# ACT fetches eight tiles instead of six in each plain run of a graph network, in bursts of six and sixteen rows

## The reference

```
edge_index = jnp.stack([src, dst])
x = _layernorm(x + _L0_gnn_ref(edge_index, x, edge_type_8, ...), axis=-1)   # message: row of x @ weight[type]
x = _layernorm(x + _L1_gnn_ref(x, edge_index, ...), axis=-1)                # message: row of x; unit length, batch norm
x = _layernorm(x + _L2_gnn_ref(x, src, dst, ...), axis=-1)                  # three attention layers, 4 heads
x = _layernorm(x + _L3_gnn_ref(x, L3_gnn_W, edge_index), axis=-1)           # message: row of (x @ W) * norm
# each message passing: agg = jax.ops.segment_sum(table[src], dst, num_segments=6250)
```

## Time and profile before

| | |
|---|---|
| median of 3 runs | 6618.36 us (6616.93 to 6622.67) |
| profiled execution | 6617.75 us, span 6615.8 us |
| busy: PE, DVE, ACT, POOL | 72%, 68%, 43%, 70% |
| run a0, first gather to last | 384.2 to 1335.4 us |
| run a1 | 1352.1 to 2301.0 us |
| run a5 | 5650.2 to 6600.5 us |

### The profile page before, as it was taken

One profiled execution on the slowest core, in us unless ns is written; L12 is line 12 of the kernel. 1 busy time (PEld: TensorE's weight loads), 2 busy tenths in 40 slices (PEclk: granted clock), 3 DMA queues, 4 the chain that ended last, 5 costly groups with the idle time before them and its releaser, 6 DMA issues. The chain is left out here.

```text
span 6615.8 us, 117241 instructions
## 1 busy us (share of the span) xinstructions
PE 4732.4 (72%) x16858; PEld 2811.9 (43%) x16858; DVE 4465.7 (68%) x11724; ACT 2869.6 (43%) x11409; POOL 4598.1 (70%) x4869
## 2 busy tenths in 40 slices
PE   9977777767677757777675777775776777667666
PEld 4445555533344334444443444443444444333333
DVE  5146555555555578888887888886888888655555
ACT  3310000000000058888875888885788887000000
POOL 0057777767777637777777777777777777677776
PEclk9988888778888777878886878877787778777777
DMA  6444444433333345555545555554455554344443
GB/s 207 158 138 123 123 123 122 122 108 109 110 109 109 106 149 141 143 143 142 144 111 139 143 144 142 143 145 147 136 142 144 143 141 114 103 116 116 115 115 107
DMA packets 448959, 865.75 MB, mean 131 GB/s; under 512 B 125022, under 2 KB 275447, under 8 KB 448219
## 3 DMA queue, kind: packets, MB, share of 16 engines
q0 software_dynamic: 227728, 627.54, 34.9%
q1 hardware_dynamic: 175408, 190.99, 9.0%
q10 hardware_dynamic: 45082, 39.73, 1.9%
HBM read 755.74 MB, written 102.10 MB: 130 GB/s over the span
## 5 line engine op out<-in xcount | busy, mean ns | idle before, releaser
L671 POOL DMA_INDIRECT rows_a<-table,rows_src x2454 | 2348.1, 957 | 874.7 <-issue 528.6
L891 PE MATMUL ps<-rows_a,hot_a 128*128 x4980 | 1865.2, 498 | 767.7 <-DMA rows_a<-table,rows_tile_a 411.2
L2080 ACT ACTIVATE rows_a<-rows_a,ex_a 128x64 f32<-128x64 f32 x9588 | 2320.8, 336 | 0.0
L2157 PE MATMUL ps<-rows_a,hot_a 128*128 128x260 f32 x4908 | 1815.9, 490 | 157.6 <-DVE agg L1989 144.3
L806 DVE TENSOR_TENSOR agg<-agg,ps 128x256 f32 (+1 forms) x2490 | 1046.0, 420 | 1203.5 <-PE ps L891 1136.5
L736 POOL DMA_INDIRECT rows_a<-table,rows_tile_a x1460 | 1383.7, 948 | 445.4 <-issue 253.2
L891 PEld LDWEIGHTS ps<-rows_a,hot_a 128*128 128x128 f32 x4980 | 1026.3, 237 | 1530.0 <-DVE agg L806 847.0
L1989 DVE TENSOR_TENSOR agg<-agg,ps 128x260 f32 x2490 | 1039.0, 417 | 320.3 <-PE ps L2157 134.1
L2157 PEld LDWEIGHTS ps<-rows_a,hot_a 128*128 128x128 f32 x4908 | 975.4, 230 | 446.9 <-issue 339.9
L736 POOL DMA_INDIRECT rows_a<-table,row x759 | 721.0, 950 | 231.7 <-issue 154.5
L2092 PE MATMUL ps<-ident,el_a 128*64 128x128 f32 x156 | 57.1, 366 | 518.1 <-DVE fac_a L1976 505.7
(11 more groups left out here) (354 smaller groups left out, 4126.9 us busy)
## 6 DMA issues: line engine op xcount, KB each, us to landing
rows_a<-table SPq DMA_DIRECT2D x6528, 1.0 KB
dstt_a<-dloc_dram SPq DMA_DIRECT2D x156, 512.0 KB
own_a<-table SPq DMA_DIRECT2D x4608, 1.0 KB
table<-ob SPq DMA_DIRECT2D x48, 1024.0 KB, 4.5
rows_a<-table,rows_src POOLq DMA_INDIRECT x2454
rows_a<-table ACTq DMA_DIRECT2D x2304, 1.0 KB
rows_a<-table,rows_tile_a POOLq DMA_INDIRECT x1460
table<-ob_n SPq DMA_DIRECT2D x98, 130.0 KB, 2.9
```

Of the source, the lines that this page charges most:

```text
L671: nc.gpsimd.indirect_dma_start(out=rows[:, n % ring, 0:width], out_offset=None, in_=table, in_offset=bass.IndirectOffsetOnAxis(ap=index[:, ...
L891: nc.tensor.matmul(ps[n % banks][:, 0:width], hot[:, m % nbuf, j, :], mine[n % 4], start=True, stop=True).then_inc(step_done, 1)
L2080: ins = nc.scalar.mul(a, a, ex[:, k % GV, s, h:h + 1])
L2157: nc.tensor.matmul(ps[j % banks][:, 0:W4], hot[:, j, :], step_rows(k, j), start=True, stop=True).then_inc(step_done, 1)
```

## The change

ACT gets eight tiles a run instead of six: every 98th from tile 84, not every 128th from tile 100. The tiles go over 12 bursts each, of 6 and 16 rows in turn (22 rows a block; the last burst of a tile has 12). Ten bursts (five blocks' worth, 110 rows) are issued ahead of the first block, not four (64 rows). In each block a burst of six stands in the middle of ACT's part, handed in as a function to the `act` methods: in a0 between the copies L974 and L978, in a1 between root and second square, in a5 between the first store and the wait for it. The burst of 16 stays behind the block. SP loads ACT's lists of row numbers at other places between its tiles, two more lists a run.

```diff
-ACT_TILE = 128
-ACT_FIRST = 100
+ACT_TILE = 98
+ACT_FIRST = 84
 ACT_TILES = tuple(range(ACT_FIRST, T - 1, ACT_TILE))
 ACT_PLACES = 2
-BURST = 16
-BURSTS_AHEAD = 4
+BURSTS = tuple((22 * b + lo, min(22 * b + hi, P)) for b in range(-(-P // 22)) for lo, hi in ((0, 6), (6, 22)))
+BLOCKS_AHEAD = 5
...
                     if i >= 2:
-                        sp.wait_ge(asked, P // BURST * (i - 1))
+                        sp.wait_ge(asked, len(BURSTS) * (i - 1))
...
-                    if ready < len(ACT_TILES) and i == (ACT_TILE * (ready - 1) + ACT_FIRST) // OWN_TILE - 1:
+                    if ready < len(ACT_TILES) and i == (ACT_TILES[ready - 2] + P // 2) // OWN_TILE:
                         ask_index_of_act(ready)
...
-                    i, lane = q * BURST // P, q * BURST % P
+                    i, (lane, end) = q // len(BURSTS), BURSTS[q % len(BURSTS)]
...
-                    ask_rows(act, mybir.EngineType.Activation, act_index[:, i % 2], lane, lane + BURST, BURST, octets, 4 * D,
+                    ask_rows(act, mybir.EngineType.Activation, act_index[:, i % 2], lane, end, end - lane, octets, 4 * D,
                              table.shape[0] - 1, rows[:, TRING + OWN_PLACES + place, 0:D], act_full[place])
                     act.sem_inc(asked, 1)
-                for _ in range(BURSTS_AHEAD):
+                for _ in range(2 * BLOCKS_AHEAD):
                     burst(0)
                 for i in range(NB):
-                    after.act(act, i)
+                    after.act(act, i, burst)
                     burst(done_by(i))
...
             nc.scalar.copy(self.xt[:, 1].rearrange("p h e -> p (h e)"), ps[4][:, 0:2 * P]).then_inc(self.xt_c, 1)
+            burst(done_by(i))
             act.wait_ge(self.l_done, i + 1)
...
             nc.scalar.sqrt(self.length[:, 0:1], self.ss[:, i:i + 1]).then_inc(self.rooted, 1)
+            burst(step)
             act.wait_ge(self.centred, i + 1)
...
                           self.ob[LAST:P, u]).then_inc(self.tail_out, 16)
+            burst(done_by(i))
             act.wait_ge(self.tail_out, 16 * (i + 1))
```

More of the change, by code:

```diff
@@ L824, in _ @@
                 after.act_first(act)
-                bursts = iter(range(len(ACT_TILES) * P // BURST))
+                bursts = iter(range(len(ACT_TILES) * len(BURSTS)))
                 def burst(done):
@@ L964, in act_x, with act @@
             nc.scalar.copy(self.xt[:, 0].rearrange("p h e -> p (h e)"), ps[4][:, 0:2 * P]).then_inc(self.xt_x, 1)
-        def act(self, act, i):
+        def act(self, act, i, burst):
             u = i % 2
```

## The result

The changed kernel takes 6645.89 us (median of 7 runs, 6640.75 to 6650.23), the kernel before 6622.42 in the runs beside them (6616.93 to 6623.02): a ratio of 1.0039, with a 95% interval of 1.0029 to 1.0049. That is 19 to 32 us slower, where +2 was forecast and 6632 was the upper end of the range. The profiled execution took 6645.88 us, 28.1 more than that of before.

What follows compares the result with a forecast made beforehand. POOL's gathers, 1.253 us a tile, were taken as the bound. Six gathers fewer (-7.5) plus stalls of 8.1, 1.4 and 0 gave +2.0 us: 6619.8 for the profiled execution, 6620.4 for the median, range 6610 to 6632.

Steps and rivals of the forecast that it cites:

- the price of the bursts ahead of block 0: ACT before its first block: ten bursts take 49.5 us, making its work 22 us later (17 to 25) in each run.
- the stalls that were worked out: POOL at tile 59 or 60 waits for PE's steps: 8.1 us in a0, 1.4 in a1, 0 in a5.
- Two gathers a run leave POOL: POOL fetches two tiles fewer in each of three runs: 6 x 1.253 = 7.5 us saved, all on the path.
- Root 0 of a0 near 448: ACT's first root in a0 moves from 426.29 to 448.3 behind the longer first bursts.
- From root 0 to the copy 9.5 us: In a0, ACT's copy of the next x follows root 0 by 9.5 us, at 457.8.
- From the copy to root 1 5.7: In a0, the burst behind the copy has 12 rows: 7.0 - 4 x 0.33 = 5.7 us, root 1 at 463.5.
- Bursts inside the blocks cost nothing: Six more rows a block, 3.0 us on ACT, are covered by its idle time in each run.
- The low clock: The longer hold starts PE at granted clock 0.50 (1.2 GHz); at full clock a0's 9.5 would be 8, stall 6.6.
- The hold is long in all three runs: Rival, 0.12: at the lower clock released PE catches up nothing; stalls 27.5 less 7.5 give +20 us, 6638.
- ACT becomes the bound: Rival, 0.07: the burst of six lifts ACT's part of a block over 19.4 us; about +33 us, 6651.
- The hold is swallowed: Rival, 0.17: DVE and PE catch up before tile 59 or 60, no stall; -7.5 us, 6611.
- More is gained than two tiles a run: Rival, 0.04: gathers get cheaper as POOL shares less; over 13.2 us needs 2.5 ns on each of 2271 gathers.

Runs made afterwards that it cites:

- Experiment 1: The changed kernel with bursts cut at multiples of four row numbers, 112 rows ahead instead of 110; ratio 1.0005 to the kernel before, +3.3 us.
- experiment 2: The changed kernel with three blocks' worth of bursts ahead (66 rows) instead of five, cuts unchanged; ratio 0.9986 to the kernel before, -9.3 us.
- experiment 3: The changed kernel with both three blocks' worth ahead (68 rows) and cuts at multiples of four; ratio 0.9985 to the kernel before, -10 us.
- experiment 6: 68 rows ahead and cuts at multiples of four, but both bursts of a block behind its part, none in its middle; ratio 0.9985 to the kernel before.
- experiment 7: Nine ACT tiles a run, ten bursts a tile cut at multiples of four, 52 rows ahead; ratio 0.9979 to the kernel before, 6619.25 against 6632.85 us.
- experiment 4: The kernel before with seven bursts of 16 ahead (112 rows) instead of four, six tiles, none in mid-block; ratio 1.0010, +6.6 us.
- experiment 5: The changed kernel with bursts cut at 5 and 22 instead of 6 and 22, 110 rows ahead; ratio 1.0069 to the kernel before, +46 us.

## Why the prediction was wrong

**The step that failed** is the price of the bursts ahead of block 0: "Five of each are 5 x 6.9 + 5 x 3.0 = 49.5, so the first block's work of ACT comes 22 us later (17 to 25 by the two bounds)". It measured 59.6, 32 us more than before. The 6.9 was that of bursts that start at multiples of 16, and I carried it over to bursts of the same length that start at 6, 50 and 94, where a burst takes 9.2 to 9.5 us (5684.17 to 5693.64 and 5707.44 to 5716.67 in the chain above). The bounds varied only the burst of six and held the other fixed, so the upper bound was no bound. The small bursts were under-priced too: taken at 3.0, with 2.0 and 3.6 as the bounds and 2.6 as another estimate, they took 3.2 to 3.8 in a5 (5680.89 to 5684.17, 5693.64 to 5697.47 above), as loads of six alone take 0.95 to 1.59. In a0 the five long bursts took 41.3 us in place of 34.5 and the five small ones 18.3 in place of 15.

**The rest of the sum stands.** Ten us more of hold on the stalls that were worked out (8.1, 1.4 and, behind 2 us of slack, 0) give 18, 11.5 and 8, in all 37.5; measured were 17.4, 13.2 and 5.1, in all 35.7. The 5.1 is less than 8 mostly because block 0 of a5 took 14.4 us from root to root (5739.81 to 5754.19 above), where 16.5 was taken. Experiment 1, where the ten bursts last the 50 us that I had taken, gives 7.7, 3.0 and 0 and +3.3 us (-2.7 to +9.3) against the forecast +2. In detail:
- Two gathers a run leave POOL: right, 757 are left and the gaps are still 1.25.
- Root 0 of a0 near 448: it came at 460.22. In experiment 1 it came at 448.20.
- From root 0 to the copy 9.5 us: 7.9. From the copy to root 1 5.7: 7.0, the same as before. In both traces the root is released by DVE (6.62 <-DVE mv_a, here and in the earlier trace rows) and not by the burst, so four rows fewer saved nothing. The prediction had read that 7.0 as the burst's own length, and its 1.65 for the reading of the numbers held a wait for DVE too. The two errors nearly cancel, 14.9 for 15.2: that is luck.
- The stall sits at tiles 59 and 60 and nowhere else: right. Most of it sat at tile 59, not 60.
- Bursts inside the blocks cost nothing: right, as far as these intervals tell (experiments 2, 3 and 6).
- The low clock: from 432 to 461 PE was busy for 0.32 us and was granted 0.50 (1.2 GHz), in the first row of the view below; in the 19 us behind it was granted 0.85 as a mean, in the second. The Trainium skill (TensorE: Matmul & The Clock Gate, Part 1) has it as a rule that activity releases the throttle; the trace agrees. But the way was 7.9 us and not 11.7 or more.

The busy time by stretch in a0 of the changed kernel (us, busy time of the engines, then granted clock, DMA share and GB/s):

```profile
432.00:461.00 29.00, 0.32 (x1) 0.00 (x0) 0.45 (x3) 1.58 (x2) 20.58 (x22) 0.50 0.41 110
461.00:480.00 19.00, 16.71 (x61) 12.27 (x62) 13.90 (x35) 1.78 (x5) 2.67 (x3) 0.85 0.13 34
```

**The rivals.** "The hold is long in all three runs" came true in its size, +20 us and more, but not by its mechanism: the steps were caught up at the pace that I had taken, and what was long was the hold itself. "ACT becomes the bound" is refuted by experiments 2 and 7. "The hold is swallowed" comes true only where the hold is short: 8.5 us more than before were swallowed (experiment 2), 20.5 more only in a5 (experiment 4, a hold of 48.2 us in a0). "More is gained than two tiles a run" is not borne out: the gathers start 1.251 us apart in both kernels, as a median.

## What to carry over

A lead that is small only at the start of a loop makes the prologue the dearest place for work that is free elsewhere: 46 rows more there cost up to 17 us a run (48 with quick loads up to 8, experiment 1), and the same rows inside the blocks nothing that could be measured. Where a price is carried over from like instructions, look at what differs in them besides the length, here the place at which they start and whether their number is a multiple of four. And a range must also vary the prices that one believes to know.

## What the runs showed of the hardware

How long a load of numbers from on-chip memory into ACT's registers takes depends on where it starts. From a place that is a multiple of four 4-byte numbers, 16 numbers took 1.25 us and 6 took 0.95 to 0.98 (the chain of a5 above). From other places 16 took 3.65 to 3.69, 17 took 3.85 to 3.89 (experiment 5) and 6 took 1.56 to 1.59. Between 6 and 16 numbers that is (3.67 - 1.57) / 10 = 0.21 us for each number off a multiple of four. The length counts too: from a multiple of four, 4 numbers took 0.49 us, 8 took 0.73 and 16 took 1.21 in experiment 1, but 6 took 0.95 in the changed kernel, more than 8 (medians of a0). That such a load goes four numbers at a time from a multiple of four, with what is left over, and all else, one by one, is my reading of these prices; they fit it (0.49 + 2 x 0.21 = 0.91 for 6), but it was not shown. In the blocks of a5, where the long bursts follow a store, the loads of 16 took longer: in the changed kernel 2.5 us from a multiple of four and 4.9 from other places, as medians. In experiment 6, where the small burst stands between the store and the long one, they took 1.23 us; why a store ahead should matter was not tested.

The Trainium skill (Runtime: NRT & Kernel Launch, Instruction fetch mechanics) puts a load of registers at about 200 ns a register; that page speaks of loads from device memory, and the lists here lie in on-chip memory. The loads from on-chip memory agree with the figure off a multiple of four (0.21 to 0.23 us a number), and on one show 1.25 us for 16, 0.08 each.
